# One row of steps over tiles for the close of a mixture of experts, a layer norm and linear attention, with plain fp32 matmuls

## The reference

```python
# layer 0, end of the second expert round: y = residual + mixed expert outputs
y = y * rsqrt(mean(y * y) + EPS) * norm_w[1]
x = x + gb * y                                   # x before the experts is kept in memory

# layer 1
h = layernorm(x) * (1 + ca) + sa
q, k, v = h @ Wq.T + bq, h @ Wk.T + bk, h @ Wv.T + bv    # 16 heads of 16
q, k = softplus(q / scale), softplus(k / scale)
kv, kn = cumsum(k[..., :, None] * v[..., None, :]), cumsum(k)   # over s
out = einsum(q, kv) / einsum(q, kn)
x = x + ga * (out @ Wo.T + bo)
```

## Time and profile before

| what | us |
|---|---|
| median of 3 runs | 2490.74 |
| lowest and highest of them | 2490.64, 2499.97 |
| the profiled execution | 2491.73 |
| its span, from the first instruction to the last | 2489.9 |
| stretch from the start of the close's first work to the last write of C | 1622.4 to 1997.3 |

### The profile page before, as it was taken

One profiled execution on the slowest core, in us unless ns is written; L12 is line 12 of the kernel. 1 busy time (PEld: TensorE's weight loads), 2 busy tenths in 40 slices (PEclk: granted clock), 3 DMA queues, 4 the chain that ended last, 5 costly groups with the idle time before them and its releaser, 6 DMA issues. The chain is left out here.

```text
span 2489.9 us, 32051 instructions
## 1 busy us (share of the span) xinstructions
PE 1854.3 (74%) x11166; PEld 1624.5 (65%) x11166; DVE 1678.5 (67%) x2776; ACT 1114.0 (45%) x2085; POOL 1055.8 (42%) x1108
## 2 busy tenths in 40 slices
PE   4799999999769799984988998603555433699990
PEld 2788888888558688773876887502444333599990
DVE  4455554454278779774878887577788877566656
ACT  4234433333134357653754666442444321466652
POOL 0232222232110146773102677621345485677755
PEclk7999999999879899996999999855777655699995
DMA  5000000000022125654320565460000012365646
GB/s 177 1 9 1 8 8 8 8 8 1 9 77 77 49 73 182 181 174 145 103 77 32 152 194 179 127 215 0 0 0 0 0 34 87 86 188 183 182 121 219
DMA packets 129533, 210.23 MB, mean 84 GB/s; under 512 B 23810, under 2 KB 96644, under 8 KB 126468
## 3 DMA queue, kind: packets, MB, share of 16 engines
q1 hardware_dynamic: 104452, 140.50, 17.4%
q0 software_dynamic: 24960, 68.19, 9.9%
HBM read 153.58 MB, written 55.05 MB: 84 GB/s over the span
## 5 line engine op out<-in xcount | busy, mean ns | idle before, releaser
L152 POOL TENSOR_TENSOR spare_g<-neg_half 128x1 f32<-128x1 f32 x96 | 28.2, 294 | 688.5 <-ACT a_sg L488 152.2
L1583 POOL DMA_INDIRECT b_kept<-sent,b_scatter_i x168 | 175.4, 1044 | 84.3 <-issue 49.4
L1576 POOL DMA_INDIRECT got<-b_rows,b_gather_i x168 | 173.5, 1033 | 72.7 <-issue 48.5
L141 PE MATMUL bank<-w_hi,m_hi 128*128 128x256 f32 x592 | 166.3, 281 | 4.0 <-DVE sent L1416 4.0
L141 PE MATMUL bank<-w_hi,m_lo 128*128 128x256 f32 x592 | 166.4, 281 | 0.0
L141 PE MATMUL bank<-w_lo,m_hi 128*128 128x256 f32 x592 | 166.0, 280 | 0.0
L141 PE MATMUL bank<-h_hi,w_hi 128*128 128x512 f32 x296 | 128.8, 435 | 38.6 <-DVE h_lo L1395 38.6
L2127 POOL DMA_INDIRECT d_kept<-d_sent,d_scatter_i x92 | 104.4, 1135 | 64.4 <-DVE d_sent L2269 43.4
L141 PE MATMUL bank<-gT_hi,w_hi 128*128 128x512 f32 x296 | 123.0, 416 | 3.2 <-DVE gT_lo L1390 3.2
L141 PE MATMUL bank<-h_hi,w_lo 128*128 128x512 f32 x296 | 121.5, 411 | 0.0
L141 PE MATMUL bank<-h_lo,w_hi 128*128 128x512 f32 x296 | 121.5, 411 | 0.0
(11 more groups left out here) (458 smaller groups left out, 6550.0 us busy)
## 6 DMA issues: line engine op xcount, KB each, us to landing
w_raw<-in_units SPq DMA_DIRECT2D x46, 512.0 KB
v_raw<-in_units SPq DMA_DIRECT2D x23, 1024.0 KB
w_raw<-in_units SPq DMA_DIRECT2D x46, 256.0 KB, 3.3
b_rows<-x SPq DMA_DIRECT2D x16, 512.0 KB, 2.9
got<-b_rows SPq DMA_DIRECT2D x16, 512.0 KB, 4.1
got<-b_kept SPq DMA_DIRECT2D x16, 512.0 KB, 5.6
close_back<-b_kept SPq DMA_DIRECT2D x16, 512.0 KB, 8.7
d_back<-d_kept SPq DMA_DIRECT2D x16, 512.0 KB, 5.4
```

Source lines behind the costliest of these rows:

```text
L141: ins = pe.matmul(out, a, b, start=first and n == 0, stop=last and n == of - 1)
L152: eng.tensor_tensor(b.spare_g[:, i:i + 1], b.neg_half[:, 0:1], b.neg_half[:, 0:1], ALU.mult)
L1576: g.indirect_dma_start(b.got[:, kg % 4, c, :], None, dram.rows[rnd], bass.IndirectOffsetOnAxis(b.gather_i[:, q:q + 1], 0)).then_inc(r.gath ...
L1583: g.indirect_dma_start(dram.kept[rnd], bass.IndirectOffsetOnAxis(b.scatter_i[:, q:q + 1], 0), b.sent[kg % 2][:, c, :], None).then_inc(r.sc ...
```

## The change

The close, the layer norm and the body become one row of 11 steps (`for i in range(NB + 3)`), written out without loops. In step i each engine handles the close's first part of tile i, the end of the close, the layer norm, q, k and the softplus of tile i - 1, the values and the quotient of tile i - 2, and the output of tile i - 3. What each engine does for which tile, in which order, stands in the four `m_` functions.

- The layer norm's subtraction and scaling go from DVE to POOL (`normalise`, four 128x256 `tensor_scalar` with two per-partition operands). The modulation by 1 + ca and sa is done by ACT as scale and bias when it takes the turned tile out of PSUM (`turned`). The turned tile is kept for one tile only, in `m_hT`.
- All products of C are plain fp32 matmuls (`plain`). The splits into high and low parts go: of the turned tile, of the weights, of q k, and of the quotient.
- q and k use two banks (2 and 3) in place of four, so the second half of q and k waits until ACT has taken the first half.
- v is made with tokens on the partitions, and its bias comes in by one fp32r matmul per chunk from a table. Denominators are one matmul per chunk and half with the product q k as the stationary operand and 8 columns. They are 128x64 values per tile. DVE copies them, takes 64 reciprocals per partition, multiplies v by the denominator and then by its reciprocal, with tokens on the partitions. TensorE turns the quotient back (8 transposes) and ACT takes it out of PSUM.
- The close's buffers are 4 in place of 8 (`CLOSE_BUFS`): the rows of tile t wait until tile t - 4 is finished. C's weights are loaded right behind the first tile's rows.

New code, cut to what matters:

```diff
+CLOSE_BUFS = 4
...
+def close_sync(sp, b, s, r, d, dram):
...
+    def old_rows(t):
+        if t >= CLOSE_BUFS:
+            sp.wait_ge(r.x.sem, r.x.at(t - CLOSE_BUFS))
         for i in range(PICKS):
-            sp.dma_start(b.close_back[t][:, i, :, :], rows_of(dram.kept[1], i * NB + t)).then_inc(r.closing[t].sem, 16)
-        sp.dma_start(b.x_old[t][:, :, :], rows_of(dram.x, t)).then_inc(r.closing[t].sem, 16)
+            sp.dma_start(b.close_back[t % CLOSE_BUFS][:, i, :, :], rows_of(dram.kept[1], i * NB + t)).then_inc(r.closing[t].sem, 16)
+        sp.dma_start(b.x_old[t % CLOSE_BUFS][:, :, :], rows_of(dram.x, t)).then_inc(r.closing[t].sem, 16)
...
+def m_scalar(act, b, s, r, p, m):
...
+    def turned(t):
+        for k in range(KD):
+            act.wait_ge(p.hT_ps.sem, p.hT_ps.at(t, k + 1))
+            act.activation(b.m_hT[:, k, :], B[2 + k][:, :], ACT.Identity, bias=b.m_cols[:, KD + k:KD + k + 1], scale=b.m_cols[:, k:k + 1]).then_inc(p.xn.sem, 1)
...
+    for i in range(NB + 3):
+        if of_iteration(i, 3) is not None:
+            output(i - 3)
+        if of_iteration(i, 1) is not None:
+            turned(i - 1)
+        if of_iteration(i, 0) is not None:
+            square_scalar(act, b, r, 1, i)
+        if of_iteration(i, 1) is not None:
+            if i == 1:
+                act.wait_ge(m.biased.sem, m.biased.at(0))
+            take(i - 1)
+            soften(i - 1)
+        if of_iteration(i + 1, 0) is not None:
+            weigh_scalar(act, b, r, 1, i + 1)
+        if of_iteration(i, 1) is not None:
+            logarithm(i - 1)
...
+    def normalise(t):
+        par = t % 2
+        if t >= 1:
+            g.wait_ge(p.hT_ps.sem, p.hT_ps.at(t - 1))
+        g.wait_ge(p.rs.sem, p.rs.at(t))
+        for c in range(CT):
+            g.tensor_scalar(b.m_hn[:, c, :], tile_of(b, t, c), b.p_mv[par][:, c, 0:1], b.p_rs2[par][:, c:c + 1], ALU.subtract, ALU.mult).then_inc(p.h.sem, 1)
...
+    for i in range(NB + 3):
+        if of_iteration(i, 2) is not None:
+            tail(i - 2, 0)
+        if of_iteration(i, 1) is not None:
+            rs(i - 1)
+            normalise(i - 1)
+        if of_iteration(i, 2) is not None:
+            tail(i - 2, 1)
+        if of_iteration(i, 0) is not None:
+            rms_gpsimd(g, b, r, 1, i)
+        if of_iteration(i, 3) is not None:
+            add(i - 3)
...
+    def divide(t):
+        if t >= 1:
+            v.wait_ge(m.outT_ps.sem, m.outT_ps.at(t - 1))
+        v.wait_ge(m.den_ps.sem, m.den_ps.at(t))
+        v.tensor_copy(b.c_den[:, :], B[4][:, 0:CT * HEADS]).then_inc(m.den.sem, 1)
+        v.wait_ge(m.den.sem, m.den.at(t))
+        v.reciprocal(b.c_rden[:, :], b.c_den[:, :]).then_inc(m.rden.sem, 1)
+        v.wait_ge(m.v_ps.sem, m.v_ps.at(t))
+        for i in range(2):
+            n = b.c_num[:, 2 * i:2 * i + 2, :]
+            v.tensor_tensor(heads(n), heads(B[6 + i][:, :].rearrange("p (c n) -> p c n", c=2)), spread(b.c_den[:, 2 * i * HEADS:(2 * i + 2) * HEADS], DH), ALU.mult).then_inc(m.num.sem, 1)
+        v.wait_ge(m.rden.sem, m.rden.at(t))
+        for i in range(2):
+            n = b.c_num[:, 2 * i:2 * i + 2, :]
+            v.wait_ge(m.num.sem, m.num.at(t, i + 1))
+            v.tensor_tensor(heads(n), heads(n), spread(b.c_rden[:, 2 * i * HEADS:(2 * i + 2) * HEADS], DH), ALU.mult).then_inc(m.out.sem, 1)
...
+    for i in range(NB + 3):
+        if of_iteration(i, 1) is not None:
+            finish(i - 1)
+            stats(i - 1)
+        if of_iteration(i, 0) is not None:
+            mix_vector(v, b, r, 1, i)
+        if i == 0:
+            prepare()
+        if of_iteration(i, 2) is not None:
+            soft(i - 2, 0)
+        if of_iteration(i, 3) is not None:
+            project(i - 3)
+        if of_iteration(i, 2) is not None:
+            soft(i - 2, 1)
+            divide(i - 2)
...
+    def plain(out, lhs, rhs, last=True):
+        for n, (a, w) in enumerate(zip(lhs, rhs)):
+            ins = pe.matmul(out, a, w, start=n == 0, stop=last and n == len(lhs) - 1)
+        return ins
...
+    def values(t):
+        if t >= 1:
+            pe.wait_ge(m.num.sem, m.num.at(t - 1))
+        for c in range(CT):
+            out = B[6 + c // 2][:, (c % 2) * D:(c % 2 + 1) * D]
+            plain(out, [h(k, c * P, P) for k in range(KD)], [W("c_wv", k) for k in range(KD)], last=False)
+            ins = pe.matmul(out, b.ones_r[:, :], b.bias_all[:, :], start=False, stop=True)
+        ins.then_inc(m.v_ps.sem, 1)
...
+    def queries(t):
+        pe.wait_ge(p.xn.sem, p.xn.at(t))
+        for o in range(KD):
+            for w, name in enumerate(C_MATS[:2]):
+                if o >= 1:
+                    pe.wait_ge(m.y.sem, m.y.at(t, 2 * o - 1 + w))
+                plain(B[2 + w][:, :], [W(name, k, o * P, P) for k in range(KD)], [h(k) for k in range(KD)]).then_inc(m.qk_ps.sem, 1)
     def denominator(t):
+        if t >= 1:
+            pe.wait_ge(m.o_taken.sem, m.o_taken.at(t - 1))
         for o in range(KD):
+            pe.wait_ge(m.qk.sem, m.qk.at(t, o + 1))
+            for c in range(CT):
+                at = c * HEADS + o * HEADS // KD
+                ins = pe.matmul(B[4][:, at:at + HEADS // KD], b.c_qk[:, o, chunk(c)], b.heads[:, 0:P:DH], start=True, stop=True)
+        ins.then_inc(m.den_ps.sem, 1)
...
+    for i in range(NB + 3):
+        if of_iteration(i, 3) is not None:
+            if i == 3:
+                pe.wait_ge(m.col.sem, m.col.at(0))
+                pe.wait_ge(s.load_c[3].sem, s.load_c[3].at(0))
+            turned_output(i - 3)
+        if of_iteration(i, 2) is not None:
+            if i == 2:
+                pe.wait_ge(s.c_w.sem, s.c_w.at(0))
+                pe.wait_ge(s.load_c[2].sem, s.load_c[2].at(0))
+            values(i - 2)
+        if of_iteration(i, 3) is not None:
+            output(i - 3)
+        if of_iteration(i, 1) is not None:
+            turned(i - 1)
+            if i == 1:
+                for sig in s.load_c[:2]:
+                    pe.wait_ge(sig.sem, sig.at(0))
+            queries(i - 1)
+        if of_iteration(i, 2) is not None:
+            denominator(i - 2)
```

## The result

The changed kernel took 2421.06 us (median of 4 runs, 2419.18 to 2424.66), the kernel before 2490.74 beside it. The ratio is 0.971, 95% interval 0.969 to 0.974: 70 us less, where 91 were forecast. The profiled execution took 2419.18 us with a span of 2417.4. These are stretches of it: C with the close merged in, all of D, and one step. Columns are as in the earlier trace rows.

A forecast was written before the change was run, and what follows sets the result against it. DVE set the pace of three stages in turn, 374.9 us. After the change a chain: 30 to the first y, 26 to the second, six steps of 31.6 (190), then 37: 283, 92 less, 2400 us; 8 in 10 for 2365 to 2440.

The forecast's parts named there:

- rival 2: TensorE's clock falls in every step: 34.4 us a step, 2422 us; at 1.2 GHz throughout 2467; chance 0.18.
- the end of the close: Sign on DVE, first in the step's chain: some 6 us in place of 2.8, stretched by POOL's first half of the tail.
- q's third bank: Sign on TensorE: the third bank of q starts right behind DVE's join of the softplus's second half.
- ScalarE's chain: Second chain of a step, over ACT from abs to q's take: 26.3 us, hidden by 5.3 us.
- the price of the normalising pass: POOL's layer norm pass taken at 0.35 us, four times 1.4 a tile, 3.7 in all with turns beside DVE.
- rival 3: Slower than before, as POOL's normalising pass is dear: gain of 92 gone at 3.2 us a pass; chance 0.04.
- The chain, member by member: A step from one quotient's end to the next, through close, layer norm, tail, join, q and k, denominators: 31.6 us.
- third and fourth of q and k: Chain member: ACT takes q's first bank, 1.0, TensorE then makes these, 3.6 + 0.2, ending at 26.2 us.
- Outside the steps: Time ahead of and behind the six steps: first y 30 us, second 26 later, 37 from the last y.
- Rival 1: DVE and POOL hardly hinder each other, so ACT's chain of 26.3 us leads: 2359 us; chance 0.18.
- Rival 4: The change doesn't overlap what it says, because a wait ties tiles together; chance 0.05 together with the unforeseen.
- roots that hold up DVE: By the exclusive lock rule, POOL's two roots of some 1 us a step hold DVE: some 8 us higher at most.

The follow-up runs named there:

- The run with constants: Changed kernel with POOL's normalising pass taking two constants in place of its two per-token columns, every wait and transfer kept: 2396.6 us, 0.961 of the kernel before.
- the run with the close first: Changed kernel with the close of all eight tiles run ahead of the row of steps, layer norm and body still merged: 2440.5 us, 0.978 of the kernel before.

## Why the prediction was right, and what it missed

**The sign, the range and the stretch** were right: 2421 lies in 2365 to 2440, and B and D stayed as they were. The single forecast, 2400, was 21 us low, and 2421 lies 1 us outside the forecast's own band (2387 to 2420, chance 0.55), in the one of rival 2 (2420 to 2440, 0.13). Of the signs, the end of the close (4.56 and 1.23 us) came as forecast. The step of 34.0 us and its granted clock of 0.75 stand where rival 2 had them, and q's third bank started 2.9 us behind the join in place of right behind it. No weighing waited for the rows of tiles 4 to 7. ScalarE's chain didn't lead: it waited 10.52 us for the transposes.

**The step that failed is the price of the normalising pass.** The prediction took 0.35 us, as nearest in kind to a pass of one operand with constants; the changed kernel has 1.21 alone and 1.66 beside DVE. That it has two scalars by partition, with no row on POOL to price it, stood in rival 3 as a risk at a chance of 0.04, with bounds up to 0.73 only. A bound from the nearest rows was no bound. By the prediction's own 8 us for each us of it, 0.87 x 4 x 8 = 28 us would be added, 2428. The run with constants took 24 us less than the changed kernel, in the stretch too. So the price is as large as the whole gap, and the rest of the sum was right to 5 us. In part that is luck: with constants the chain up to the join was 1.1 us a step shorter than forecast, and the way from the join to the last of q and k, for which the forecast's chain had no slow clock, 0.8 longer.

**The chain, member by member**, from the end of the quotient at 1788.5 us, forecast and measured: end of the close 6.3 and 5.7; root 9.7 and 9.6; normalising 14.8 and 16.5; second half of the tail 18.9 and 20.1; join's add 21.4 and 22.7; third and fourth of q and k 26.2 and 29.1; denominators and quotient 31.6 and 34.1. Two members are off. Normalising is late by 1.7 us, less than its price would give, because less waiting for DVE comes on top: 1.8 us (6.64 where 4.84 is the price of four), where 3.7 were forecast. And q and k are late by another 1.6, which is not in this chain: TensorE pauses for 5.59 us for the late tile, its clock is at half behind the pause, and TensorE's own half of the way, tile to transposes to q, is last in place of the join. Filling the pause took just this 1.6 back.

**Outside the steps** it was 5 us: the first y was complete at 1654.8, 32.4 us behind 1622.4 (30 forecast), the second 28.0 behind it (26), and the end 38.0 us behind the last (37). Six steps gave 14.

**Rival 1**, no hindrance: wrong. The tail and its turns cost 3.4 us a step, and the normalising passes' own turns 1.8 (6.64 less 4.84). **Rival 2**, the falling clock: its size was right by chance (34.4 a step and 2422). Its cause was only in part what it said. The transposes and q's first bank ran at 1.2 GHz behind a pause, and where the pause was filled, they ran at full clock. Filling took 1.6 us off a step and the cheap pass 3.2, so neither is the other's whole. The pause was longer by the dear pass (5.59 us), but with the cheap one (3.27 us) the same bank ran at half speed too. The quotient's transposes were at half speed, as it had them (1.97 us, 1.09 at full clock). Values and Wo, which it had at half speed throughout, were at full speed from the third chunk of the values on: 1.91 us for the first chunk's matmuls, 1.28, then 1.02, and 3.72 for all 16 of Wo. **Rival 4** didn't occur. The price that the prediction set on a rule, roots that hold up DVE, didn't occur either: beside POOL's root at 1796.99 DVE's mix took its usual 1.64 us. The other way round they did wait: POOL's root for the close took 1.19 and 1.48 us beside DVE's join.

**Where the 70 us come from.** Running the close by itself costs 16 to 19, as many and as large reciprocals as before cost 33 to 34. The rest, some 17 to 21 us, is left to all else that the change does, the layer norm and the splits taken off DVE above all; no run tells them apart, nor what plain matmuls cost or gave. The parts don't add up strictly, since each changes what the others hide behind.

## What to carry to other kernels

Once no engine is busy for more than three quarters of a step, price the chain, and treat any form of instruction that the trace doesn't hold as unknown: moving a pass to an idle engine can treble its price, and the nearest row in size says nothing of a form with other operands. Two engines that hinder each other want their passes in different parts of a step; here passes with one tensor operand were held up too. Which of them runs first was worth some 7 us here (2387 to 2380, by two orders changed together), filling TensorE's pauses 9 in the changed kernel and nothing that the times show elsewhere. Look for the pause that a late producer makes on TensorE: in the changed kernel it was paid once as waiting and again at the lower clock, and empty work in it shows the price of the second part without touching anything else.

## What the runs showed of the hardware

- A 128x256 fp32 pass with two scalars by partition takes 1.21 us on GpSimd, 0.40 on VectorE, and some 0.5 on ScalarE; with constants GpSimd takes 0.40.
- Many short passes suffer much from the turns: four of 0.40 us on GpSimd lasted 4.36 beside four VectorE passes of 1.2 to 1.4 and 0.8, about one VectorE pass for each.
- VectorE's passes with one tensor operand in SBUF and two scalars by partition wait for GpSimd as well: four of 0.41 us lasted 4.21 beside GpSimd's 1.22 and 2.34.
- Even GpSimd's 128x4 passes wait: 1.19 and 1.48 us beside VectorE's join, where 0.19 and 1.04 are the times beside an idle VectorE (in the run with the close first).
- Useless matmuls in a pause of TensorE took 1.6 us off each step: the granted clock behind the pause was 1.00 with them and 0.50 without.
